# Turning the token rows of a sparse expert block: two TensorE transposes into one half of PSUM and two ScalarE copies, or four TensorE matmuls into both halves and one copy

## The chip, the cores and the metric

The kernel runs on one core of a Trainium2 chip. The metric is the time of one execution on the device in microseconds (us), as the median of several runs. The engines are named as in the profile: PE is TensorE's matmuls, PEld its weight loads, DVE is VectorE, ACT is ScalarE, POOL is GpSimd, SP is SyncE.

## What is computed

The model is a chain of eight stages on a tensor of 8 x 32 x 32 pixels with 64 channels: a spatial stage and then a mixture of experts, four times over. The change lies in the last two mixtures, `ffn2` and `ffn3`, which compute the same function with different weights. Each normalised token goes to the best two of eight experts; an expert is a gated network of width 682:

```python
    def _L2_ffn_ref(x, router_w, w1, w2, w3):
        N_EXPERTS = 8
        TOP_K = 2
        B, T, C = x.shape
        flat = x.reshape(-1, C)
        logits = flat @ router_w.T
        probs = jax.nn.softmax(logits, axis=-1)
        topk_probs, topk_idx = jax.lax.top_k(probs, TOP_K)
        topk_probs = topk_probs / (jnp.sum(topk_probs, axis=-1, keepdims=True) + 1e-09)
        onehot = jax.nn.one_hot(topk_idx, N_EXPERTS, dtype=flat.dtype)
        gates = jnp.einsum('nk,nke->ne', topk_probs, onehot)
        h1 = jnp.einsum('nc,ehc->neh', flat, w1)
        h3 = jnp.einsum('nc,ehc->neh', flat, w3)
        h = jax.nn.silu(h1) * h3
        y = jnp.einsum('neh,ech->nec', h, w2)
        out = jnp.einsum('ne,nec->nc', gates, y)
        return out.reshape(B, T, C)
...
    x = x + _L2_conv_ref(_ln_c(x), ...)
    t = _to_tokens(x)
    t = t + _L2_ffn_ref(_ln_t(t), L2_ffn_router_w, L2_ffn_w1, L2_ffn_w2, L2_ffn_w3)
    x = _from_tokens(t, x)
    x = x + _L3_conv_ref(_ln_c(x), ...)
    t = _to_tokens(x)
    t = t + _L3_ffn_ref(_ln_t(t), L3_ffn_router_w, L3_ffn_w1, L3_ffn_w2, L3_ffn_w3)
```

## The kernel before

Both stages are built by `sparse_stage`. Its first part normalises the tokens, chooses experts and scatters every token's row, with its gate, into regions of DRAM by expert. Its second part, the one that the change touches, works through `SLOT_BLOCKS` = 71 blocks of 256 rows, each block with one expert's weights; there are 142 blocks in the two stages. All operands are float32.

A block b is done in these steps, with the line numbers of the profile:

- `turn_x` (L1251): the 256 rows lie in `xin` as two tiles of 128 rows by 64 channels. Each tile is transposed on TensorE, with the identity as moving operand, into the PSUM tile `x_ps`, partitions 0 to 63. The rows are the stationary operand.
- `copy_x` (L1310 and L1311): ScalarE copies those 64 partitions twice into `turned` in SBUF, once to partitions 0 to 63 and once to 64 to 127. Both halves are needed because the two up-projections, w1 and w3, lie in the two halves of the partitions of `weights` and are multiplied by the two halves of TensorE's rows.
- `up(b, c)` for c = 0, 1, 2 (L1262): each call is four matmuls of 64 rows by 114 columns, with 256 moving columns: two chunks of hidden units, and for each w1 and w3.
- ScalarE takes Silu of the first product (L1320) and VectorE multiplies it by the second (L1350), which gives `hidden`.
- `downs(b)` (L1273): six matmuls of 114 rows by 64 columns, alternately into partitions 0 to 63 and 64 to 127 of `y_ps`. VectorE copies the sums to `y_half` (L1331).
- `fold(b)` (L1284): two matmuls of the full array that turn the result back and add the halves; VectorE multiplies by the gates (L1338), and GpSimd scatters the rows to DRAM (L1241).

The order on TensorE is written out by hand: for each b it is `up(b, 0)`, `up(b, 1)`, `turn_x(b + 1)`, `fold(b - 2)`, `up(b, 2)`, `downs(b - 1)`. On ScalarE the copy for block b + 1 stands between the Silu of c = 1 and that of c = 2. `up(b, 0)` waits for `x_copied`, `up(b, c)` for the `hidden` of two steps before, since there are two PSUM buffers.

In the trace an `up`, `downs` or `fold` matmul shows as two MATMUL records, each with its own weight load, and a transpose as one: L1251 has 284 records for 284 transposes, L1284 has 568 for 284 matmuls. "128*64" in a row is rows by columns of the array that are in use, "128x128" behind it the moving operand.

Of the kernel before, what the change touches and what calls it, by code (L numbers as in the profile page):

```python
# [15 lines left out]
P = 128  # L16
BATCH, SIDE, CH = 8, 32, 64
# [731 lines left out]
BLOCK = SUB * P  # L749
HELD = 26  # L750
# [56 lines left out]
def sparse_stage(nc, sem, k, name):  # L807
    dram = k.dram
    blocks_of_rows = k.slots.rearrange("(b p j) c -> b p j c", p=P, j=SUB)
    with ExitStack() as ctx:  # L810
# [18 lines left out]
        with ExitStack() as inner:  # L829
            def sbi(n, shape, dt=F32):  # L830
                return inner.enter_context(nc.sbuf_tensor(f"{name}_{n}", shape, dt))

            def psi(n, shape):
                return inner.enter_context(nc.psum_tensor(f"{name}_{n}", shape, F32))
# [14 lines left out]
            turned, kept, multiplied, placed, rows_set = (  # L849
                sem(f"{name}_{n}") for n in ("turned", "kept", "multiplied", "placed", "rows_set"))  # L850
# [304 lines left out]
        with ExitStack() as inner:  # L1155
# [3 lines left out]
            def psi(n):  # L1159
# [4 lines left out]
            x_ps, out_ps = psi("x_ps"), psi("out_ps")  # L1164
            y_ps = [psi(f"y_ps{i}") for i in (0, 1)]
            xin = sbi("xin", [P, HELD, SUB, ROW])
            turned = sbi("turned", [P, 2, BLOCK])
# [7 lines left out]
            x_turned, x_copied, up_done, silu_done, hidden_done = (  # L1175
                sem(f"{name}_{n}") for n in ("x_turned2", "x_copied", "up_done", "silu_done", "hidden_done"))
# [69 lines left out]
            @block.tensor  # L1246
            def _(pe):
                def turn_x(b):
                    pe.wait_ge(x_loaded[b % HELD], 16 * (b // HELD + 1))
                    for j in range(SUB):  # L1250
                        last = nc.tensor.transpose(x_ps[0:CH, j * P:(j + 1) * P], xin[:, b % HELD, j, 0:CH],  # L1251
                                                   k.ident[:, :])
                    last.then_inc(x_turned, 1)

                def up(b, c):
                    n = PAIRS_C * b + c
                    if n >= 2:
                        pe.wait_ge(hidden_done, n - 1)
                    for chunk in (2 * c, 2 * c + 1):
                        for w in (0, 1):  # L1260
                            rows_of = slice(w * CH, (w + 1) * CH)
                            last = nc.tensor.matmul(up_ps[w][n % 2][0:SIZE,  # L1262
                                                                    chunk % 2 * BLOCK:(chunk % 2 + 1) * BLOCK],
                                                    weights[rows_of, b % WEIGHTS, chunk * SIZE:(chunk + 1) * SIZE],
                                                    turned[rows_of, b % 2, :], start=True, stop=True)
                    last.then_inc(up_done, 1)

                def downs(b):
                    pe.wait_ge(hidden_done, PAIRS_C * (b + 1))
                    for c in range(CHUNKS):  # L1270
                        half = c % 2
                        col = UP_COLS + c * CH
                        last = nc.tensor.matmul(y_ps[b % 2][half * CH:(half + 1) * CH, 0:BLOCK],  # L1273
                                                weights[0:SIZE, b % WEIGHTS, col:col + CH],
                                                hidden[0:SIZE, b % 2, c // 2, c % 2 * BLOCK:(c % 2 + 1) * BLOCK],
                                                start=(c < 2), stop=(c >= CHUNKS - 2))
                    last.then_inc(down_done, 1)

                def fold(b):
                    pe.wait_ge(y_kept, b + 1)  # L1280
                    if b > 0:
                        pe.wait_ge(y_ready, b)
                    for j in range(SUB):
                        last = nc.tensor.matmul(out_ps[:, j * CH:(j + 1) * CH],  # L1284
                                                y_half[:, b % 2, j * P:(j + 1) * P], k.fold[:, :],
                                                start=True, stop=True)
                    last.then_inc(folded, 1)

                turn_x(0)
                for b in range(SLOT_BLOCKS):  # L1290
                    pe.wait_ge(x_copied, b + 1)
                    pe.wait_ge(w_loaded[b % WEIGHTS], 16 * (b // WEIGHTS + 1))
                    up(b, 0)
                    up(b, 1)
                    if b + 1 < SLOT_BLOCKS:
                        turn_x(b + 1)
                    if b >= 2:
                        fold(b - 2)
                    up(b, 2)
                    if b >= 1:  # L1300
                        downs(b - 1)
                downs(SLOT_BLOCKS - 1)
                fold(SLOT_BLOCKS - 2)
                fold(SLOT_BLOCKS - 1)

            @block.scalar
            def _(act):
                def copy_x(b):
                    act.wait_ge(x_turned, b + 1)
                    nc.scalar.copy(turned[0:CH, b % 2, :], x_ps[0:CH, 0:BLOCK])  # L1310
                    nc.scalar.copy(turned[CH:P, b % 2, :], x_ps[0:CH, 0:BLOCK]).then_inc(x_copied, 1)  # L1311

                copy_x(0)
                for b in range(SLOT_BLOCKS):
                    for c in range(PAIRS_C):
                        n = PAIRS_C * b + c
                        act.wait_ge(up_done, n + 1)
                        if n >= 2:
                            act.wait_ge(hidden_done, n - 1)
                        nc.scalar.activation(silu[0:SIZE, n % 2, :], up_ps[0][n % 2][0:SIZE, :],  # L1320
                                             ACT.Silu).then_inc(silu_done, 1)
                        if c == 1 and b + 1 < SLOT_BLOCKS:
                            copy_x(b + 1)
# [1939 lines left out]
```

## Time and profile before

| | |
|---|---|
| median of 3 runs | 2289.25 us (2287.74 to 2291.01) |
| time of the profiled execution | 2279.4 us |
| span of the profile | 2277.6 us |
| mean granted TensorE clock (1.0 is full speed) | 0.839 |
| PE busy | 1677.3 us (74%), 11157 records |
| PEld busy | 967.5 us (42%) |
| DVE busy | 1245.0 us (55%) |
| ACT busy | 965.8 us (42%) |
| L1262 PE, `up` | 445.8 us busy, 3408 records |
| L1273 PE, `downs` | 215.2 us busy, 1704 records |
| L1284 PE, `fold` | 79.7 us busy, 568 records |
| L1251 PE, `turn_x` | 58.6 us busy, 284 records |
| L1310 ACT, the first copy | 50.1 us busy, 142 |

The profile is of one execution, whose time is 2 us more than its span and 10 us less than the median. Busy shares are means over eight unlike stages; what the change is worth is read from the blocks, whose turns run from 1273.1 us, at the start of `ffn2`, to 2236.1 us, in `ffn3`, with the `sht` stage between. Ends of matmuls in the trace are modelled, so durations of neighbouring groups overlap; starts are the better measure.

### The profile page before, as it was taken

How to read it: one execution, taken by the hardware profiler on the slowest of the kernel's cores; microseconds unless marked ns; L12 is line 12 of the kernel's file. 1: busy time of each engine (PE TensorE's matmuls, PEld its weight loads, DVE VectorE, ACT ScalarE, POOL GpSimd, SP SyncE). 2: the span in 40 equal slices, each digit the busy share in tenths (PEclk: the TensorE clock that was granted, in tenths of full speed). 3: DMA queues.
4: the chain of work that ended last, by engine and by line, in shares of the span. 5: the costliest groups of instructions: out<-in, count | busy, mean ns of one | idle time of the engine just before them, and what ended most of it. 6: DMA issues, size and time to landing. Idle time of an engine off the chain costs nothing. (4 is left out here: it accounts for less than half of the span.)

```text
span 2277.6 us, 30440 instructions
## 1 busy us (share of the span) xinstructions
PE 1677.3 (74%) x11157; PEld 967.5 (42%) x11157; DVE 1245.0 (55%) x2416; ACT 965.8 (42%) x1715; POOL 590.1 (26%) x591
## 2 busy tenths in 40 slices
PE   2899996897999970312304599999845539999994
PEld 2433333345333340100103366666545426666663
DVE  6643335655633357578787555555462565555554
ACT  2565653333655543325123244444322424444441
POOL 0100000001000000000005577743452157776332
PEclk8899997996999975556555799999967759999997
DMA  1322210002222200000000354444268014544444
GB/s 41 76 68 65 65 56 20 0 0 50 76 65 65 65 23 0 0 0 0 0 4 27 117 147 147 149 138 134 92 152 167 7 57 149 147 146 143 133 133 151
DMA packets 117333, 175.30 MB, mean 77 GB/s; under 512 B 38106, under 2 KB 66522, under 8 KB 116674
## 3 DMA queue, kind: packets, MB, share of 16 engines
q1 hardware_dynamic: 99906, 155.38, 23.8%
q0 software_dynamic: 17280, 17.99, 2.4%
q8 instruction: 89, 1.46, 0.3%
q14 instruction: 58, 0.48, 0.1%
HBM read 148.60 MB, written 24.70 MB: 76 GB/s over the span
## 5 line engine op out<-in xcount | busy, mean ns | idle before, releaser
L1350 DVE TENSOR_TENSOR ffn_hidden<-ffn_silu,ffn_up_ps 114x512 f32<-114x512 f32 x426 | 293.0, 688 | 349.9 <-ACT ffn_silu L1320 349.0
L1262 PE MATMUL ffn_up_ps<-ffn_turned,ffn_weights 64*114 64x256 f32 x3408 | 445.8, 394 | 5.8 <-DMA ffn_weights<-in_ffn_weights 4.9
L1320 ACT ACTIVATE ffn_silu<-ffn_up_ps 114x512 f32<-114x512 f32 x426 | 254.4, 597 | 388.9 <-PE ffn_up_ps L1262 386.5
L826 POOL DMA_INDIRECT slots<-ffn_rows,ffn_slot x256 | 251.7, 983 | 557.4 <-DVE ffn_slot L944 386.4
L736 ACT ACTIVATE ffn_hidden<-ffn_up_ps,ffn_b 128x512 f32<-128x512 f32 x512 | 310.1, 689 | 198.0 <-PE ffn_up_ps L631 198.0
L1241 POOL DMA_INDIRECT results<-ffn_yout,ffn_xin x284 | 271.9, 957 | 246.0 <-DVE ffn_yout L1338 179.6
L1262 PEld LDWEIGHTS ffn_up_ps<-ffn_turned,ffn_weights 64*114 64x114 f32 x3408 | 288.1, 176 | 110.6 <-issue 59.6
L631 PE MATMUL ffn_up_ps<-ffn_T,ffn_up_w 64*128 64x512 f32 x1024 | 261.2, 623 | 3.1 <-ACT ffn_hidden L736 3.1
L652 PE MATMUL ffn_y_ps<-ffn_hidden,ffn_down 128*64 128x512 f32 x1024 | 247.9, 605 | 3.4 <-DVE ffn_y_total L526 3.4
L1273 PE MATMUL ffn_y_ps<-ffn_hidden,ffn_weights 114*64 114x256 f32 x1704 | 215.2, 388 | 0.0
L526 DVE SCALAR_TENSOR_TENSOR ffn_gated<-ffn_y_ps,ffn_b,ffn_gates 128x512 f32<-128x512 f32 x96 | 72.0, 751 | 204.7 <-PE ffn_y_ps L652 203.1
L631 PEld LDWEIGHTS ffn_up_ps<-ffn_T,ffn_up_w 64*128 64x128 f32 x1024 | 91.5, 188 | 168.5 <-ACT ffn_hidden L736 92.9
L1273 PEld LDWEIGHTS ffn_y_ps<-ffn_hidden,ffn_weights 114*64 114x64 f32 x1704 | 109.7, 136 | 89.9 <-DVE ffn_hidden L1350 48.2
L652 PEld LDWEIGHTS ffn_y_ps<-ffn_hidden,ffn_down 128*64 128x64 f32 x1024 | 62.3, 136 | 161.6 <-ACT ffn_hidden L736 85.3
L1251 PE MATMUL ffn_x_ps<-ident,ffn_xin 128*64 128x128 f32 x284 | 58.6, 289 | 48.0 <-DMA ffn_xin<-slots 48.0
L526 DVE SCALAR_TENSOR_TENSOR ffn_y_total<-ffn_y_ps,ffn_b,ffn_gates 128x512 f32<-128x512 f32 x32 | 23.7, 750 | 113.4 <-PE ffn_y_ps L652 92.0
L1057 PE MATMUL ffn_turn_ps<-ident,D 128*128 128x128 f32 x64 | 17.3, 431 | 89.8 <-DVE D L879 89.8
L1284 PE MATMUL ffn_out_ps<-fold,ffn_y_half 128*128 128x64 f32 x568 | 79.7, 263 | 1.4 <-DVE ffn_y_half L1331 1.4
L1284 PEld LDWEIGHTS ffn_out_ps<-fold,ffn_y_half 128*128 128x128 f32 x568 | 74.6, 191 | 3.2 <-DVE ffn_y_half L1331 1.7
L2724 POOL MEMSET hyp_ones<- 128x128 f32 x1 | 0.2, 204 | 288.7 <-POOLq L3096 288.7
L2138 PE MATMUL dc_conv_ps<-dc_fresh,dc_step_w 128*128 128x512 f32 x144 | 67.6, 617 | 8.8 <-DVE dc_fresh L2124 8.8
L1310 ACT COPY ffn_turned<-ffn_x_ps 64x256 f32<-64x256 f32 x142 | 50.1, 353 | 56.0 <-PE ffn_x_ps L1251 56.0
(412 smaller groups left out, 2067.1 us busy)
## 6 DMA issues: line engine op xcount, KB each, us to landing
ffn_weights<-in_ffn_weights SPq DMA_DIRECT2D x142, 534.0 KB
ffn_gates<-gate_rows SPq DMA_DIRECT2D x128, 256.0 KB
ffn_xin<-slots SPq DMA_DIRECT2D x142, 66.0 KB
sht_mix<-in_sht_weights SPq DMA_DIRECT2D x8, 1024.0 KB, 8.4
results<-ffn_yout,ffn_xin POOLq DMA_INDIRECT x284
slots<-ffn_rows,ffn_slot POOLq DMA_INDIRECT x256
D<-results SPq DMA_DIRECT2D x16, 256.0 KB, 5.4
ffn_second<-results SPq DMA_DIRECT2D x16, 256.0 KB, 5.9
```

What stands on the lines that cost most here:

```text
L526: nc.vector.scalar_tensor_tensor(target, y_ps[th][:, :], b2[:, p:p + 1], gates[:, n % GATES, th, :], ALU.add, ALU.mult).then_inc(y_gated, 1)
L631: nc.tensor.matmul(up_ps[j][:, :], up_w[rows, 2 * p + half, c * P:(c + 1) * P], T[rows, g * NTOK:(g + 1) * NTOK], start=True, stop=True).t ...
L652: last = nc.tensor.matmul(y_ps[th][rows, :], down[:, 2 * p + half, c, :], hidden[:, n % 2 * UNITS + 2 * half + th, :], start=(c == 0), sto ...
L736: nc.scalar.activation(hidden[:, n % 2 * UNITS + j, :], up_ps[j][:, :], ACT.Gelu, bias=b1[:, bias_at:bias_at + 1], scale=1.0).then_inc(hid ...
L826: nc.gpsimd.indirect_dma_start(k.slots, bass.IndirectOffsetOnAxis(slot[c][:, t:t + 1], 0), rows[c][:, t, :], None).then_inc(row_stored[h], 16)
L1241: nc.gpsimd.indirect_dma_start(k.results, bass.IndirectOffsetOnAxis(xin[:, b % HELD, j, CH + 1:CH + 2].bitcast(I32), 0), yout[:, b % HELD, ...
L1262: last = nc.tensor.matmul(up_ps[w][n % 2][0:SIZE, chunk % 2 * BLOCK:(chunk % 2 + 1) * BLOCK], weights[rows_of, b % WEIGHTS, chunk * SIZE:( ...
L1273: last = nc.tensor.matmul(y_ps[b % 2][half * CH:(half + 1) * CH, 0:BLOCK], weights[0:SIZE, b % WEIGHTS, col:col + CH], hidden[0:SIZE, b % ...
L1284: last = nc.tensor.matmul(out_ps[:, j * CH:(j + 1) * CH], y_half[:, b % 2, j * P:(j + 1) * P], k.fold[:, :], start=True, stop=True)
L1320: nc.scalar.activation(silu[0:SIZE, n % 2, :], up_ps[0][n % 2][0:SIZE, :], ACT.Silu).then_inc(silu_done, 1)
L1350: nc.vector.tensor_tensor(hidden[0:SIZE, b % 2, c, :], silu[0:SIZE, n % 2, :], up_ps[1][n % 2][0:SIZE, :], ALU.mult).then_inc(hidden_done, 1)
L2138: last = nc.tensor.matmul(bank[:, :], step_w[:, g, dx, :], fresh[slot][:, :, dx:dx + SIDE], start=False, stop=(dx == 2), skip_group_check= ...
```

## The change

`turn_x` issues an ordinary matmul with the identity in place of each transpose, and issues it twice, with the output in partitions 0 to 63 and in 64 to 127 of `x_ps`. `copy_x` then copies all 128 partitions in one instruction.

```diff
                 def turn_x(b):
                     pe.wait_ge(x_loaded[b % HELD], 16 * (b // HELD + 1))
                     for j in range(SUB):
-                        last = nc.tensor.transpose(x_ps[0:CH, j * P:(j + 1) * P], xin[:, b % HELD, j, 0:CH],
-                                                   k.ident[:, :])
+                        for half in (0, 1):
+                            last = nc.tensor.matmul(x_ps[half * CH:(half + 1) * CH, j * P:(j + 1) * P],
+                                                    xin[:, b % HELD, j, 0:CH], k.ident[:, :], start=True, stop=True)
                     last.then_inc(x_turned, 1)
...
                 def copy_x(b):
                     act.wait_ge(x_turned, b + 1)
-                    nc.scalar.copy(turned[0:CH, b % 2, :], x_ps[0:CH, 0:BLOCK])
-                    nc.scalar.copy(turned[CH:P, b % 2, :], x_ps[0:CH, 0:BLOCK]).then_inc(x_copied, 1)
+                    nc.scalar.copy(turned[:, b % 2, :], x_ps[:, 0:BLOCK]).then_inc(x_copied, 1)
```

On TensorE's queue a block now reads like this, from the turn for block 12 in `ffn2` to the last `up` of block 11; names in brackets are the semaphores that a row waits for, and "64x128" is the output's shape:

```order
L1251 MATMUL ffn_x_ps<-ident,ffn_xin 64x128 [waits ffn2_x_loaded12]
L1251 MATMUL ffn_x_ps<-ident,ffn_xin 64x128
L1284 MATMUL ffn_out_ps<-fold,ffn_y_half 128x64 [waits ffn2_y_ready,ffn2_y_kept]
L1284 MATMUL ffn_out_ps<-fold,ffn_y_half 128x64
L1262 MATMUL ffn_up_ps<-ffn_turned,ffn_weights 114x256 [waits ffn2_hidden_done]
L1262 MATMUL ffn_up_ps<-ffn_turned,ffn_weights 114x256 x3
```

The same place in the changed kernel, whose lines are numbered one higher:

```order
L1252 MATMUL ffn_x_ps<-ident,ffn_xin 64x128 [waits ffn2_x_loaded12]
L1252 MATMUL ffn_x_ps<-ident,ffn_xin 64x128 x3
L1285 MATMUL ffn_out_ps<-fold,ffn_y_half 128x64 [waits ffn2_y_ready,ffn2_y_kept]
L1285 MATMUL ffn_out_ps<-fold,ffn_y_half 128x64
L1263 MATMUL ffn_up_ps<-ffn_turned,ffn_weights 114x256 [waits ffn2_hidden_done]
L1263 MATMUL ffn_up_ps<-ffn_turned,ffn_weights 114x256 x3
```

Two instructions have become four ahead of the fold; the order around them, and what each row waits for, is the same.

## Rows read from the trace of the kernel before

**Rows 1.** The page: PE's busy tenths in 40 slices, and the last chain by engine.

```profile
PE   2899996897999970312304599999845539999994
...
PE 16%; DMA 1%; DVE 0%; SPq 0%; issue 0%; POOL 0%; POOLq 0%; ACT 0%
```

**Rows 2.** Busy time by engine in ten blocks of `ffn3`, with the clock.

```profile
core 0: us, PE busy (x) PEld busy (x) DVE busy (x) ACT busy (x) POOL busy (x), PEclk, DMA share, GB/s
1889.34:1940.81 51.47, 51.47 (x422) 34.48 (x422) 26.89 (x50) 24.06 (x50) 38.97 (x42) 1.00 0.51 147
```

**Rows 3.** Timeline of PE, one block: start, duration to the modelled end, what.

```profile
1930.44 1.99 PE L1262 MATMUL ffn_up_ps<-ffn_turned,ffn_weights 64*114 64x256 f32 x16
1932.36 0.41 PE L1251 MATMUL ffn_x_ps<-ident,ffn_xin 128*64 128x128 f32 x2
1932.61 0.56 PE L1284 MATMUL ffn_out_ps<-fold,ffn_y_half 128*128 128x64 f32 x4
1933.09 1.12 PE L1262 MATMUL ffn_up_ps<-ffn_turned,ffn_weights 64*114 64x256 f32 x8
1934.14 1.52 PE L1273 MATMUL ffn_y_ps<-ffn_hidden,ffn_weights 114*64 114x256 f32 x12
1935.59 1.99 PE L1262 MATMUL ffn_up_ps<-ffn_turned,ffn_weights 64*114 64x256 f32 x16
```

**Rows 4.** Timeline of ACT in the same block; idle time before a row in brackets.

```profile
1932.97 0.35 ACT L1310 COPY ffn_turned<-ffn_x_ps 64x256 f32<-64x256 f32 x1
1933.34 0.36 ACT L1311 COPY ffn_turned<-ffn_x_ps 64x256 f32<-64x256 f32 x1
1934.26 0.60 ACT L1320 ACTIVATE ffn_silu<-ffn_up_ps 114x512 f32<-114x512 f32 x1 [0.56 <-PE ffn_up_ps L1262]
```

**Rows 5.** Timeline of DVE in the same block: `hidden` of c = 0.

```profile
1932.24 0.69 DVE L1350 TENSOR_TENSOR ffn_hidden<-ffn_silu,ffn_up_ps 114x512 f32<-114x512 f32 x1 [1.26 <-ACT ffn_silu L1320]
```

**Rows 6.** Timeline of PE, `ffn2`'s last block, which has no turn.

```profile
1639.35 0.66 PE L1284 MATMUL ffn_out_ps<-fold,ffn_y_half 128*128 128x64 f32 x4
1639.97 1.12 PE L1262 MATMUL ffn_up_ps<-ffn_turned,ffn_weights 64*114 64x256 f32 x8
1641.02 3.00 PE L1273 MATMUL ffn_y_ps<-ffn_hidden,ffn_weights 114*64 114x256 f32 x24
1643.96 0.66 PE L1284 MATMUL ffn_out_ps<-fold,ffn_y_half 128*128 128x64 f32 x4
```

**Rows 7.** Timeline of PE in `ffn0`: full-array matmuls, then column halves.

```profile
126.39 2.00 PE L664 MATMUL ffn_out_ps<-fold,ffn_y_total 128*128 128x64 f32 x16
128.32 1.08 PE L652 MATMUL ffn_y_ps<-ffn_hidden,ffn_down 128*64 128x512 f32 x4
```

**Rows 8.** Timeline of PE in the `sht` stage: transposes (L1861) and matmuls (L1871).

```profile
1779.47 0.60 PE L1861 MATMUL sht_modes_ps<-ident,sht_lat 128*128 128x128 f32 x4
1779.90 1.06 PE L1871 MATMUL sht_out_ps<-sht_inverse,sht_modes 128*128 128x128 f32 x8
1780.80 0.60 PE L1861 MATMUL sht_modes_ps<-ident,sht_lat 128*128 128x128 f32 x4
```

**Rows 9.** Four lines on PE: duration of one record, ns, min/median/max.

```profile
L1251 PE MATMUL ffn_x_ps<-ident,ffn_xin x284: 272/297/423, 1273.1 to 2236.1; 128*64 128x128 f32 x142
...
L1273 PE MATMUL ffn_y_ps<-ffn_hidden,ffn_weights x1704: 379/379/431, 1286.0 to 2245.5; 114*64 114x256 f32 x190
...
L1801 PE MATMUL sht_spec_ps<-sht_forward_leg,sht_fourier x256: 270/273/445, 1697.4 to 1744.7; 128*32 128x128 f32 x128
...
L652 PE MATMUL ffn_y_ps<-ffn_hidden,ffn_down x1024: 592/592/886, 88.5 to 816.0; 128*64 128x512 f32 x171
```

**Rows 10.** Timeline of PE at the start of `ffn2`.

```profile
1276.19 3.76 PE L1262 MATMUL ffn_up_ps<-ffn_turned,ffn_weights 64*114 64x256 f32 x16 [2.48 <-DMA ffn_weights<-in_ffn_weights]
...
1284.63 0.41 PE L1251 MATMUL ffn_x_ps<-ident,ffn_xin 128*64 128x128 f32 x2
1284.97 1.12 PE L1262 MATMUL ffn_up_ps<-ffn_turned,ffn_weights 64*114 64x256 f32 x8
```

## The prediction

> **What bounds the kernel now.** I read the page first: PE shows nine tenths or more through both stretches of blocks, and the last chain is 16% PE against 1% for anything else [rows 1]. A busy PE can still hide waiting, so I went to the windows: in ten blocks of `ffn3` PE is busy for all 51.47 us at full clock (1.00, the 2.4 GHz level), DVE and ACT for about half of it [rows 2]. So a block takes 5.15 us, as the starts of two neighbouring blocks say too, 1930.44 and 1935.59 [rows 3]. Both other engines wait for PE: ACT stood idle for 0.56 us until the Silu of c = 2 had its product [rows 4], and DVE for 1.26 us behind ACT [rows 5]. What counts is therefore the time that TensorE's queue takes, piece by piece, and the timeline of PE gives it by starts: `up` 1.92, turn 0.25 (1932.36 to 1932.61), fold 0.48 (to 1933.09), `up` 1.05, `downs` 1.45 [rows 3].
>
> **What the rows say about the array.** Three things are needed to price the new turn.
>
> First, a slot. Sixteen `up` records take 1.99 us and eight take 1.12 [rows 3], so eight take 0.87. Alone on the full array, matmul records of 128 columns follow each other every 0.11 us (eight from 1779.90 to 1780.80) and transposes every 0.108 (four from 1779.47 to 1779.90) [rows 8]. Records of 256 columns should need 0.217 each, 1.74 for eight; they need half, because w1 and w3 sit in different row halves and run side by side. So a slot of 256 columns is 0.217 us and one of 128 is 0.109.
>
> Second, whether column halves overlap too, which the new turn needs. `ffn0` has the same pattern: four records of 512 columns, one matmul to each column half, take 1.08 us [rows 7]. A record lasts 0.592 [rows 9] and its slot is 4 x 0.109 = 0.436; one after another the last would end at 3 x 0.436 + 0.592 = 1.90, in two slots at 0.436 + 0.592 = 1.03. It is two slots, plus 0.05 for a first weight load that nothing hides. `downs` agrees: five slots of 0.217 and a last record of 0.379 [rows 9] make 1.46, measured 1.52 [rows 3], so 0.06 for that load.
>
> Third, the change of shape. Where row halves, column halves and the full array follow each other, the next group starts 0.06 to 0.08 us before the modelled end of the last record: `up` to turn (1930.44 + 1.99 against 1932.36), fold to `up`, `downs` to `up` [rows 3], full array to column halves (126.39 + 2.00 against 128.32) [rows 7], column halves to fold (1641.02 + 3.00 against 1643.96) [rows 6]. I call this a drain and use 0.07. Today the turn passes to the fold without one: the fold starts 0.16 before the turn's modelled end and takes 0.56 in all [rows 3], and so do transposes and full-array matmuls in `sht` (1779.47 + 0.60 against 1779.90) [rows 8]. After a drain a fold takes 0.66 [rows 6], because its first weight load is no longer covered.
>
> **The change part by part.** Removed on PE: two transposes, one record each. Added: four matmuls of two records, so eight records of 128 columns, four in each column half, in four slots. From the turn's start: 0.06 for the first load, three slots of 0.109, then the last record. Its length is that of a 128-column record in column tiles, 0.27 (the median of L1801; the shortest of L1251 is the same) [rows 9]. That is 0.66 to its modelled end; less 0.07, the fold starts 0.59 after the turn, where it starts 0.25 after it now. The drain ahead of the turn is there already and stays. The fold comes after a drain now: 0.66 less 0.07, so the next `up` starts 0.59 after it, where it is 0.48 now. Turn and fold together: 0.59 + 0.59 = 1.18, now 0.73, so **0.45 us more per block**.
>
> Each stage has 70 turns in its loop, and 68 of them stand before a fold: 136 x 0.45 = 61.2 us. The first two turns in each loop have no fold behind them. At the warm one `up` starts 0.34 after the turn [rows 10], and it would be 0.59 then; four times 0.25 is 1 us, somewhat more where the clock is still low. The turn ahead of each loop costs nothing: `up` waits 2.48 us for its weights there [rows 10], and the added matmuls, about half a microsecond at the low clock, fit in.
>
> Removed on ACT: one copy of 0.36 us in each block [rows 4], 51 us in all. I put this at nothing. The second copy ends at 1933.70 [rows 4] and the `up` that needs it starts at 1935.59 [rows 3], 1.89 later; ACT is idle for half of a block and its next Silu waits for PE in any case. The copy of 128 partitions is not in the trace; between nothing and twice the present 0.36 it ends long before that `up`. Behind it on ACT stands the Silu of c = 2, which will be 0.45 later with PE. The other waits get slacker: `up(b, 2)` needs the `hidden` that ends at 1932.93 [rows 5] and starts at 1933.09 [rows 3], so PE is the later already, and nothing is added for DVE, GpSimd or the DMAs.
>
> Sum: 61.2 + 1 = 62 us. The profiled execution took 2279.4, so it would take 2341.6. The median is 10 us above that execution, and I add the same 62 to it: **2351 us**, 2.7% slower. A change under 0.2%, some 5 us, could not be told from none.
>
> **A rule weighed against the rows.** An ordinary matmul streams two records where a transpose streams one, at equal 0.11 per 128 columns [rows 8]: twice the time. The Trainium skill, page "TensorE: Matmul & The Clock Gate", section "Terms", says that transpose mode is four times faster for FP32. By that the four matmuls would need eight slots even with both halves side by side, and the total would be that of the second rival; the rows bear out twice, so the sum stays.
>
> **The rivals.**
> - No drain behind the turn, as with the transposes today. Then the fold starts after 0.06 + 4 x 0.109 = 0.50 and takes 0.48: 0.25 more per block, 35 us, 2324 us. Against it: column halves to fold does drain [rows 6]. A matmul with the identity that is run as a transpose all the same, one record per half, comes to nearly the same: 0.06 + 0.109 + 0.27 - 0.07 + 0.59 = 0.96, 0.23 more, 2321 us. Nothing in the rows speaks for it.
> - The halves do not overlap, as each matmul to half 64 to 127 stands behind one that reads the same rows as weights. Eight slots in place of four add 4 x 0.109 = 0.44: 0.89 per block, 122 us, 2411 us. Against it: the same alternation in `ffn0` and in `downs` [rows 3, 7].
> - Not slower: the x copies set the start of the next block. Then the turn's end, 0.34 later, is paid back by one copy of 0.36: 0.02 less per block, 2286 us, no change that can be told. It decides only where the second copy ends later than `downs`, so it would have to be 1.9 us later than it is [rows 3, 4].
>
> **How the numbers follow.** The forecast gets 0.80; slot, load and drain are each known to about 0.01 us, so with some play for the first blocks and for the step from the profiled execution to a median it reaches from 2342 to 2362. The cheaper turn gets 0.08, the dearer one 0.09 (0.02 of it for the rule of four), the copies 0.03. The range 2330 to 2370 takes the whole of the first and room for a drain or a load of half or twice the size, and leaves the three others out, 0.20 together. Slower: 0.80 + 0.08 + 0.09 = 0.97; same 0.02 and faster 0.01 share the last.
>
> **What would show it.** In the profile after: 1136 records on the turn's line in place of 284, about 0.27 us each; a block of 5.60 us on PE's timeline; the fold 0.59 after the turn, starting about 0.07 before its modelled end, and 0.66 long; clock 1.00 in the blocks; one copy of 128x256 per block, ACT's busy time some 50 us less, and its idle time before the Silu of c = 2 about 0.7 longer. A fold that starts before the last turn record is 0.2 old would show the first rival, starts of the two halves 0.11 apart and never together the second. What would make the forecast wrong: PE idle inside a block today that the modelled ends hide, or a shape of matmul that drains between its own halves.

## The result and the profile after

The changed kernel takes 2349.66 us, the median of four runs (2348.55 to 2352.92), against 2289.25 before: a ratio of 1.027, with a 95% interval of 1.0256 to 1.0285. The forecast was 2351 us, slower. Ratios and their intervals, here and below, are estimates from all the runs and not quotients of two medians, from which they differ a little. A fourth run of the kernel before took 7328.6 us, far from all others, and is not in its median.

The page of the changed kernel: busy time by engine, PE's tenths in 40 slices, the last chain by engine, and the lines of the turn, the fold and the copy (busy time, mean ns of one, idle time before).

```profile
PE 1747.8 (74%) x12009; PEld 1014.2 (43%) x12009; DVE 1244.5 (53%) x2416; ACT 928.5 (39%) x1573; POOL 589.6 (25%) x591
...
PE   2899996888999941211223999999665539999994
...
PE 17%; DMA 1%; DVE 0%; SPq 0%; issue 0%; POOL 0%; POOLq 0%; ACT 0%
...
L1252 PE MATMUL ffn_x_ps<-ident,ffn_xin 128*64 128x128 f32 x1136 | 94.8, 288 | 48.1 <-DMA ffn_xin<-slots 48.1
...
L1285 PE MATMUL ffn_out_ps<-fold,ffn_y_half 128*128 128x64 f32 x568 | 93.5, 287 | 1.4 <-DVE ffn_y_half L1331 1.4
...
L1311 ACT COPY ffn_turned<-ffn_x_ps 128x256 f32<-128x256 f32 x142 | 52.8, 372 | 57.5 <-PE ffn_x_ps L1252 57.5
```

PE is as full as before, 74% of a longer span, and still holds the chain [rows 1]. The turn's line has 1136 records where 284 stood, and the fold's line, which was not edited, went from 79.7 to 93.5 us. To put the place of the loss beyond doubt, here are the two stretches of blocks, each from its first turn into its last fold, in windows with the busy time of the engines, the clock and the DMA share. First the changed kernel:

```profile
core 0: us, PE busy (x) PEld busy (x) DVE busy (x) ACT busy (x) POOL busy (x), PEclk, DMA share, GB/s
...
1281.92:1685.40 403.48, 399.83 (x3408) 265.67 (x3408) 190.64 (x354) 154.18 (x285) 221.75 (x233) 0.99 0.41 128
1918.30:2321.30 403.00, 399.13 (x3408) 265.29 (x3408) 190.66 (x354) 154.18 (x285) 221.67 (x232) 0.99 0.42 128
```

And the same two stretches of the kernel before:

```profile
1273.07:1645.70 372.63, 368.87 (x2981) 246.20 (x2982) 190.77 (x354) 172.28 (x356) 221.85 (x233) 0.99 0.45 139
1875.75:2247.50 371.75, 368.30 (x2981) 245.78 (x2982) 190.75 (x354) 172.21 (x356) 221.66 (x232) 0.99 0.45 139
```

The stretches grew by 30.85 and 31.25 us, 62.1 together, at the same mean granted clock of 0.99. PE's busy time in them grew by 30.96 and 30.83, so nothing of this is a new wait. ACT has 18 us less to do in each, and the time does not show it.

The timeline of PE in the changed kernel, at the start of `ffn2`, to be laid beside [rows 10], and in one block, beside [rows 3]:

```profile
1285.42 3.76 PE L1263 MATMUL ffn_up_ps<-ffn_turned,ffn_weights 64*114 64x256 f32 x16 [2.38 <-DMA ffn_weights<-in_ffn_weights]
...
1293.87 0.66 PE L1252 MATMUL ffn_x_ps<-ident,ffn_xin 128*64 128x128 f32 x8
1294.45 1.12 PE L1263 MATMUL ffn_up_ps<-ffn_turned,ffn_weights 64*114 64x256 f32 x8
...
1938.46 1.99 PE L1263 MATMUL ffn_up_ps<-ffn_turned,ffn_weights 64*114 64x256 f32 x16
1940.37 0.66 PE L1252 MATMUL ffn_x_ps<-ident,ffn_xin 128*64 128x128 f32 x8
1940.96 0.66 PE L1285 MATMUL ffn_out_ps<-fold,ffn_y_half 128*128 128x64 f32 x4
1941.55 1.12 PE L1263 MATMUL ffn_up_ps<-ffn_turned,ffn_weights 64*114 64x256 f32 x8
1942.60 1.52 PE L1274 MATMUL ffn_y_ps<-ffn_hidden,ffn_weights 114*64 114x256 f32 x12
1944.05 1.99 PE L1263 MATMUL ffn_up_ps<-ffn_turned,ffn_weights 64*114 64x256 f32 x16
```

In the block, by starts: `up` 1.91, turn 0.59 (was 0.25), fold 0.59 (was 0.48), `up` 1.05, `downs` 1.45. A block takes 5.59 us where it took 5.15. The turn ends 0.07 after the fold's start, and the fold takes 0.66 in all, as after column halves in [rows 6]. At the start, `up` follows the warm turn after 0.58 (was 0.34), and the wait for weights still covers the turn ahead of the loop, 2.38 us where it was 2.48.

The timeline of ACT in that block, to be laid beside [rows 4]:

```profile
1940.49 0.60 ACT L1320 ACTIVATE ffn_silu<-ffn_up_ps 114x512 f32<-114x512 f32 x1 [0.27 <-PE ffn_up_ps L1263]
1941.08 0.37 ACT L1311 COPY ffn_turned<-ffn_x_ps 128x256 f32<-128x256 f32 x1
1942.72 0.60 ACT L1320 ACTIVATE ffn_silu<-ffn_up_ps 114x512 f32<-114x512 f32 x1 [1.27 <-PE ffn_up_ps L1263]
```

One copy of 128 partitions takes 0.37, hardly longer than one of 64 did (0.35 and 0.36). The time that it saves went straight into the wait for the next product, together with PE's delay: 1.27 us where 0.56 stood.

### The profile page after: what moved, and what is told of

It reads as the page before. It is cut to its first block and busy times, and to the rows that moved or that the text cites. A ratio compares the mean times of both kernels' runs of the same rounds, so it can differ in the third digit from the quotient of the medians.

```text
span 2351.0 us, 32002 instructions
## 1 busy us (share of the span) xinstructions
PE 1747.8 (74%) x12009; PEld 1014.2 (43%) x12009; DVE 1244.5 (53%) x2416; ACT 928.5 (39%) x1573; POOL 589.6 (25%) x591
## 5 line engine op out<-in xcount | busy, mean ns | idle before, releaser
L652 PE MATMUL ffn_y_ps<-ffn_hidden,ffn_down 128*64 128x512 f32 x1024 | 247.8, 605 | 3.5 <-DVE ffn_y_total L526 3.5
L652 PEld LDWEIGHTS ffn_y_ps<-ffn_hidden,ffn_down 128*64 128x64 f32 x1024 | 62.4, 136 | 161.5 <-ACT ffn_hidden L736 85.4
L1252 PE MATMUL ffn_x_ps<-ident,ffn_xin 128*64 128x128 f32 x1136 | 94.8, 288 | 48.1 <-DMA ffn_xin<-slots 48.1
L1252 PEld LDWEIGHTS ffn_x_ps<-ident,ffn_xin 128*64 128x64 f32 x1136 | 60.0, 137 | 98.9 <-DMA ffn_xin<-slots 50.4
L1285 PE MATMUL ffn_out_ps<-fold,ffn_y_half 128*128 128x64 f32 x568 | 93.5, 287 | 1.4 <-DVE ffn_y_half L1331 1.4
L1311 ACT COPY ffn_turned<-ffn_x_ps 128x256 f32<-128x256 f32 x142 | 52.8, 372 | 57.5 <-PE ffn_x_ps L1252 57.5
```

The costliest lines, as they stand in the source:

```text
L652: last = nc.tensor.matmul(y_ps[th][rows, :], down[:, 2 * p + half, c, :], hidden[:, n % 2 * UNITS + 2 * half + th, :], start=(c == 0), sto ...
L1252: last = nc.tensor.matmul(x_ps[half * CH:(half + 1) * CH, j * P:(j + 1) * P], xin[:, b % HELD, j, 0:CH], k.ident[:, :], start=True, stop=True)
L1285: last = nc.tensor.matmul(out_ps[:, j * CH:(j + 1) * CH], y_half[:, b % 2, j * P:(j + 1) * P], k.fold[:, :], start=True, stop=True)
```

## The experiments

The theory: PE alone sets the time of a block. A slot is the time from the start of one record to that of the next on the same part of the array. Half of the loss is slots (four of 128 columns where two were), the other half the change of shape between the turn and the fold, with the uncovered weight loads on both sides of it; the second half of the partitions and the copies weigh nothing. The rivals of the prediction split the same sum in other ways: halves one behind the other, a turn without a drain, copies that matter.

**The copy alone.** The transposes stay, and one copy takes all 128 partitions. The upper half of `x_ps` is filled only once, with block 0's rows, and holds them for all later blocks; so the time is that of the copy edit, but the w3 products are those of block 0's rows. The diff is against the kernel before.

```diff
...
                     for j in range(SUB):
+                        if b == 0:
+                            nc.tensor.matmul(x_ps[CH:P, j * P:(j + 1) * P], xin[:, b % HELD, j, 0:CH],
+                                             k.ident[:, :], start=True, stop=True)
                         last = nc.tensor.transpose(x_ps[0:CH, j * P:(j + 1) * P], xin[:, b % HELD, j, 0:CH],
...
                     act.wait_ge(x_turned, b + 1)
-                    nc.scalar.copy(turned[0:CH, b % 2, :], x_ps[0:CH, 0:BLOCK])
-                    nc.scalar.copy(turned[CH:P, b % 2, :], x_ps[0:CH, 0:BLOCK]).then_inc(x_copied, 1)
+                    nc.scalar.copy(turned[:, b % 2, :], x_ps[:, 0:BLOCK]).then_inc(x_copied, 1)
```

> ScalarE's part of the change alone: the two transposes stay, one copy of 128 partitions replaces the two copies. It leaves out that the second half of the copied rows is that of their block: it holds block 0's rows throughout, so the products with w3 are wrong. My theory: the copies end 1.89 us before the matmul that needs them, so a block stays at 5.15 us and the time at 2290 us, within 3 us. The rival, that the copies set the start of the next block: 0.36 us less in each of 142 blocks, 51 us, 2239 us.

Measured: 2289.01 us (ten runs, 2280.08 to 2290.81) against 2288.11 before, ratio 1.0003 (0.9986 to 1.0019). Its timeline of ACT, one copy and the Silu behind it:

```profile
1942.92 0.37 ACT L1313 COPY ffn_turned<-ffn_x_ps 128x256 f32<-128x256 f32 x1
1944.21 0.60 ACT L1322 ACTIVATE ffn_silu<-ffn_up_ps 114x512 f32<-114x512 f32 x1 [0.92 <-PE ffn_up_ps L1265]
```

The copy that fell away, 0.36 us, came back as wait: the Silu waits 0.92 us for PE where it waited 0.56 [rows 4]. So the ScalarE half of the change, done without the other, is worth nothing that can be measured: the rival of copies that matter, 2239 us, is out.

**The matmuls alone.** The four matmuls of the changed kernel, with the two copies of the kernel before. The diff is against the changed kernel, here and in the next three.

```diff
-                    nc.scalar.copy(turned[:, b % 2, :], x_ps[:, 0:BLOCK]).then_inc(x_copied, 1)
+                    nc.scalar.copy(turned[0:CH, b % 2, :], x_ps[0:CH, 0:BLOCK])
+                    nc.scalar.copy(turned[CH:P, b % 2, :], x_ps[0:CH, 0:BLOCK]).then_inc(x_copied, 1)
```

> TensorE's part of the change alone: four matmuls into both halves, but the two copies of before, both from the lower half, so that the upper half of the PSUM tile is written for nothing. My theory: the time of the changed kernel, 2350 us within 3, with a block of 5.59 us, since the saved copy pays nothing there either. The rival, that the saved copy pays for part of the matmuls: up to 51 us more than the changed kernel, 2400 us.

Measured: 2349.59 us (2346.88 to 2351.29), ratio 1.0262 (1.0243 to 1.0281). That is the changed kernel's time, and PE's timeline is the changed kernel's too (turn to fold 0.59, fold to `up` 0.59, a block 5.59). The whole loss is TensorE's.

**Two matmuls, to one half.** The matmuls to the upper half are left out, and the two copies are back.

```diff
-                        for half in (0, 1):
-                            last = nc.tensor.matmul(x_ps[half * CH:(half + 1) * CH, j * P:(j + 1) * P],
-                                                    xin[:, b % HELD, j, 0:CH], k.ident[:, :], start=True, stop=True)
+                        last = nc.tensor.matmul(x_ps[0:CH, j * P:(j + 1) * P], xin[:, b % HELD, j, 0:CH],
+                                                k.ident[:, :], start=True, stop=True)
...
-                    nc.scalar.copy(turned[:, b % 2, :], x_ps[:, 0:BLOCK]).then_inc(x_copied, 1)
+                    nc.scalar.copy(turned[0:CH, b % 2, :], x_ps[0:CH, 0:BLOCK])
+                    nc.scalar.copy(turned[CH:P, b % 2, :], x_ps[0:CH, 0:BLOCK]).then_inc(x_copied, 1)
```

> Only the transposes replaced: two ordinary matmuls into the lower half in place of two transposes, and the two copies of before. My theory: the four records in one column half need the same four slots as four records in each of two, and the drain ahead of the fold is there too, so it is as slow as the changed kernel, 2350 us, with a turn of 0.59 us and a fold of 0.66. The rival, that the second half costs slots of its own: about half of the added time, 2320 us.

Measured: 2346.65 us (2340.11 to 2351.27), ratio 1.025 (1.0221 to 1.0278), an interval that overlaps the changed kernel's. Its timeline of PE:

```profile
1940.65 0.65 PE L1251 MATMUL ffn_x_ps<-ident,ffn_xin 128*64 128x128 f32 x4
1941.23 0.66 PE L1284 MATMUL ffn_out_ps<-fold,ffn_y_half 128*128 128x64 f32 x4
1941.82 1.12 PE L1262 MATMUL ffn_up_ps<-ffn_turned,ffn_weights 64*114 64x256 f32 x8
```

Four records take 0.65 us where eight take 0.66. The second half is free within 0.01 us, and the prediction's second rival (halves one behind the other) is out. It also says where the loss begins: with the step from a transpose to a matmul, even with as many instructions as before and in the same half.

**Slots without the change of shape.** Each transpose is issued twice into the same place, with the two copies. That makes four records of 128 columns per block, as many slots as the changed kernel's eight records in two halves take.

```diff
-                        for half in (0, 1):
-                            last = nc.tensor.matmul(x_ps[half * CH:(half + 1) * CH, j * P:(j + 1) * P],
-                                                    xin[:, b % HELD, j, 0:CH], k.ident[:, :], start=True, stop=True)
+                        for again in (0, 1):
+                            last = nc.tensor.transpose(x_ps[0:CH, j * P:(j + 1) * P], xin[:, b % HELD, j, 0:CH],
+                                                       k.ident[:, :])
...
-                    nc.scalar.copy(turned[:, b % 2, :], x_ps[:, 0:BLOCK]).then_inc(x_copied, 1)
+                    nc.scalar.copy(turned[0:CH, b % 2, :], x_ps[0:CH, 0:BLOCK])
+                    nc.scalar.copy(turned[CH:P, b % 2, :], x_ps[0:CH, 0:BLOCK]).then_inc(x_copied, 1)
```

> Slots without the drain: each transpose of the kernel before is issued twice, to the same place, so four records of 128 columns in four slots, in the shape that passes to the fold without a drain. My theory: 2 more slots of 0.109 us per block and nothing else, 0.22 in 140 turns, 31 us, 2320 us, with the fold still 0.48 ahead of the next up. The rival, that all of the change's cost is slots and a drain is free: 0.45 per block, 2350 us.

Measured: 2321.51 us (2319.19 to 2323.96), ratio 1.0141 (1.0121 to 1.0162). Its timeline of PE:

```profile
1941.32 0.63 PE L1252 MATMUL ffn_x_ps<-ident,ffn_xin 128*64 128x128 f32 x4
1941.78 0.56 PE L1285 MATMUL ffn_out_ps<-fold,ffn_y_half 128*128 128x64 f32 x4
1942.27 1.12 PE L1263 MATMUL ffn_up_ps<-ffn_turned,ffn_weights 64*114 64x256 f32 x8
...
1946.69 0.63 PE L1252 MATMUL ffn_x_ps<-ident,ffn_xin 128*64 128x128 f32 x4
```

The turn is about as long as in the changed kernel (0.63 against 0.66), but the fold starts 0.46 after it and not 0.59, and needs 0.49 and not 0.59: it starts 0.17 before the modelled end of the turn, and its first load lies under the turn (the weight load starts at 1941.68, 0.10 ahead of the fold's first record; in the changed kernel it starts with the fold, at 1940.96). A block takes 5.37. So of the 0.44 us that a block lost, 0.22 are two more slots and 0.22 the change of shape with its loads. In the total: 33 us of slots (2321.51 less 2288.11), 28 of the rest (2349.59 with the matmuls alone, less 2321.51).

**The matmuls where the shape does not change.** The changed kernel's turn is put behind `downs`, which also writes to column halves, two blocks ahead; the copy moves with it, and on SP's queue the rows are loaded ahead of the weights.

```diff
...
-                        load_weights(experts[b - first], b)
                         if b > 0:
                             load_x(places[b - first], b)
+                        load_weights(experts[b - first], b)
...
                 turn_x(0)
+                pe.wait_ge(x_copied, 1)
+                turn_x(1)
                 for b in range(SLOT_BLOCKS):
...
                     up(b, 1)
-                    if b + 1 < SLOT_BLOCKS:
-                        turn_x(b + 1)
                     if b >= 2:
...
                         downs(b - 1)
+                    if b + 2 < SLOT_BLOCKS:
+                        pe.wait_ge(x_copied, b + 2)
+                        turn_x(b + 2)
...
```

> The drain of the change undone by place: the four matmuls of the changed kernel stand right behind the down-projections, which use the same column halves, and turn two blocks ahead; the fold stands alone between the ups. (Rows are loaded ahead of the weights of the same block, so that they are there.) My theory: no drain between downs and turn, whose first weight load is covered, so the turn costs its four slots, 0.44 us; the fold keeps its drains, and the up behind it waits 0.03 for the product of c = 0, as in the block without a turn today. A block of 1.92 + 0.62 + 1.05 + 1.45 + 0.44 = 5.48 us, 0.33 over the kernel before, 46 us, 2335 us. The rival, that place does not matter and only the added records cost: a block of 5.59 us, 2350 us.

Measured: 2332.85 us (2330.28 to 2335.64) against 2286.92 before, ratio 1.0213 (1.0183 to 1.0242). Its timeline of PE:

```profile
1945.09 1.99 PE L1263 MATMUL ffn_up_ps<-ffn_turned,ffn_weights 64*114 64x256 f32 x16
1947.01 0.66 PE L1285 MATMUL ffn_out_ps<-fold,ffn_y_half 128*128 128x64 f32 x4
1947.64 1.12 PE L1263 MATMUL ffn_up_ps<-ffn_turned,ffn_weights 64*114 64x256 f32 x8
1948.69 1.52 PE L1274 MATMUL ffn_y_ps<-ffn_hidden,ffn_weights 114*64 114x256 f32 x12
1950.03 0.61 PE L1252 MATMUL ffn_x_ps<-ident,ffn_xin 128*64 128x128 f32 x8
1950.57 1.99 PE L1263 MATMUL ffn_up_ps<-ffn_turned,ffn_weights 64*114 64x256 f32 x16
```

The turn starts 1.34 after `downs`, where `up` started 1.45 after it, and takes 0.61 where it took 0.66, with its first load covered. A block takes 5.48 us (1945.09 to 1950.57), 0.11 less than in the changed kernel, and the kernel loses 46 us and not 60. The same instructions, one change of shape fewer. Behind `downs` the turn starts 0.18 before the modelled end of the last record, so an ordinary matmul does not drain where the shape stays. The price of a change is not one number, though: this block has as many slots and as many changes as the one with doubled transposes and takes 0.11 more (5.48 against 5.37), mostly because the fold, now behind an `up`, takes 0.63 by starts and not 0.49.

**The kernel before with fewer changes of shape.** If a change costs 0.12 us or so, the kernel before pays for four in each block. Here its transposes and copies stay, and blocks go in pairs, so that `downs` stands between two `up` and the turns and folds of two blocks stand together: six changes in two blocks where eight were. `x_ps` and `out_ps` hold two blocks, `turned` three, and the rows are loaded ahead of the weights. ScalarE's and VectorE's orders, not shown, follow. The diff is against the kernel before.

```diff
...
+                for b in range(1, SLOT_BLOCKS, 2):
+                    start(b)
                     up(b, 0)
                     up(b, 1)
-                    if b + 1 < SLOT_BLOCKS:
-                        turn_x(b + 1)
-                    if b >= 2:
-                        fold(b - 2)
+                    downs(b - 1)
                     up(b, 2)
-                    if b >= 1:
-                        downs(b - 1)
+                    start(b + 1)
+                    up(b + 1, 0)
+                    if b + 2 < SLOT_BLOCKS:
+                        turn_x(b + 2)
+                        turn_x(b + 3)
+                    if b >= 2:
+                        fold(b - 2, b - 2)
+                    fold(b - 1, b - 2)
+                    up(b + 1, 1)
+                    up(b + 1, 2)
+                    downs(b)
...
```

> The lesson turned round, from the kernel before with its transposes and two copies: fewer changes of shape. Blocks go in pairs: up(b,0) up(b,1), downs(b-1), up(b,2) up(b+1,0), both turns and both folds of a pair together, up(b+1,1) up(b+1,2), downs(b); so six changes of shape in two blocks where there are eight. My theory, from starts in the trace: a pair takes 3 x 1.92 for the ups, 2 x 1.45 for the downs, and 0.47 + 0.93 for four transposes and eight fold records, 10.06 us where two blocks take 10.29; 35 pairs in each stage save 16 us, 2273 us. The rival, that a drain costs nothing and records alone count: the same 2289 us. A third: the rows or products of a pair come too late and the ups wait, which would show as idle PE, and slower than before.

Measured: 2278.93 us (twelve runs, 2269.76 to 2286.55) against 2286.92 before (seventeen runs), ratio 0.997 (0.9954 to 0.9987). It is faster than the kernel before, but by 8 us only, where its forecast had 16. Its timeline of PE: a turn in `ffn2` for which the rows came late, with the `up` behind it; a pair as most are in `ffn3`; and one there in which the rows came late.

```profile
1410.13 0.41 PE L1251 MATMUL ffn_x_ps<-ident,ffn_xin 128*64 128x128 f32 x2 [2.39 <-DMA ffn_xin<-slots]
...
1411.31 1.99 PE L1262 MATMUL ffn_up_ps<-ffn_turned,ffn_weights 64*114 64x256 f32 x16
...
1942.18 0.62 PE L1251 MATMUL ffn_x_ps<-ident,ffn_xin 128*64 128x128 f32 x4
1942.65 1.00 PE L1284 MATMUL ffn_out_ps<-fold,ffn_y_half 128*128 128x64 f32 x8
1943.58 1.99 PE L1262 MATMUL ffn_up_ps<-ffn_turned,ffn_weights 64*114 64x256 f32 x16
1945.50 1.52 PE L1273 MATMUL ffn_y_ps<-ffn_hidden,ffn_weights 114*64 114x256 f32 x12
1946.94 1.99 PE L1262 MATMUL ffn_up_ps<-ffn_turned,ffn_weights 64*114 64x256 f32 x16
1948.86 1.52 PE L1273 MATMUL ffn_y_ps<-ffn_hidden,ffn_weights 114*64 114x256 f32 x12
1950.31 1.99 PE L1262 MATMUL ffn_up_ps<-ffn_turned,ffn_weights 64*114 64x256 f32 x16
1952.22 0.63 PE L1251 MATMUL ffn_x_ps<-ident,ffn_xin 128*64 128x128 f32 x4
...
2006.04 0.41 PE L1251 MATMUL ffn_x_ps<-ident,ffn_xin 128*64 128x128 f32 x2 [2.78 <-DMA ffn_xin<-slots]
2006.29 1.20 PE L1284 MATMUL ffn_out_ps<-fold,ffn_y_half 128*128 128x64 f32 x8
2007.42 3.42 PE L1262 MATMUL ffn_up_ps<-ffn_turned,ffn_weights 64*114 64x256 f32 x16
```

A pair takes 10.04 us (1942.18 to 1952.22) where two blocks took 10.29: 0.25 less for two changes fewer, so 0.12 each, near the 0.11 that the run before saved by one, and about half of the 0.22 that the change between turn and fold costs. Over 70 pairs that would be 17 us. Part of it is lost where the second turn of a pair has to wait for its rows: 2.39 us once in `ffn2`, 2.78 once in `ffn3`. Both times the rows are those of block 26, by the order of the loads, and a pair turns that block one block earlier than before. The chain that led to the second wait shows why they were late:

```profile
1995.01 2.41 DMA slots<-ffn_rows,ffn_slot
...
1998.46 2.70 SPq L1192
...
2001.18 2.77 SPq L1192
...
2004.13 1.86 DMA ffn_xin<-slots
```

SP's queue waited for the last scatter into `slots` before it loaded the rows of block 25; then it read its tables of places and experts for the next 13 blocks (L1192, 2.70 and 2.77 us), and only then asked for block 26, whose rows took 1.86 us to land. The second wait costs more than itself, as the windows around it show, the first of them in the wait:

```profile
2004.00:2006.00 2.00, 0.00 (x0) 0.00 (x0) 0.29 (x1) 0.00 (x0) 1.70 (x2) 1.00 0.44 120
2007.42:2010.70 3.28, 3.28 (x17) 2.35 (x16) 1.04 (x3) 1.16 (x3) 2.45 (x3) 0.55 0.15 50
2012.00:2014.00 2.00, 2.00 (x20) 1.37 (x16) 0.63 (x2) 0.60 (x1) 1.39 (x3) 1.00 0.37 110
```

Behind it the mean granted clock is 0.55, almost all of it at the 1.2 GHz level, and the same 16 records take 3.42 us in place of 1.99; then it is 1.00 again. Behind the wait of 2.39 in `ffn2` it is not so: there the 16 records take 1.99. From the first turn to the start of the last fold the two stages take 366.1 and 367.2 us, against 372.3 and 371.4 before: 10.3 of the 17 us. The two waits, that slow group and two shorter waits for rows (0.39 and 0.26) are 7.2 us, which covers what is missing. A version that keeps the pairs and has these rows loaded earlier was not tried, nor was the new order on SP's queue alone.

## Why the prediction was right

**PE sets the time.** It does: the stretches of blocks grew by as much as PE's busy time in them, and one copy in place of two, taken alone, changed nothing.

**The slot and the column halves.** The turn was to start its fold after 0.59 us and did. Two halves to a slot, read from `ffn0` [rows 7], is shown by the run with two matmuls, where half the records took the same time.

**The drain.** This was the disputed step: today the turn passes to the fold without one, and the same row shape, 128*64, stands before both. The forecast said that the turn as a matmul in a column half would drain like `downs` before a fold [rows 6]. The doubled transposes show it: with as many slots, 0.22 us per block hang on which instruction stands ahead of the fold. That it is the shape and not the matmul as such is shown by the turn behind `downs`, which starts 0.18 before the modelled end, and by [rows 8], where full-array matmuls pass to transposes 0.16 before theirs. The forecast's two prices came out as well: 0.34 us more at the turn and 0.11 at the fold.

The Trainium skill, page "TensorEngine Tiling (Array Packing)", section "Key Properties", says that changing the tiling mode drains the engine. The trace agrees: a step between row halves, column halves and the full array costs 0.11 to 0.22 us here, drain and uncovered weight load together. The Trainium skill, page "TensorEngine Tiling (Array Packing)", section "Restrictions", says that column tiling rules out the FP32 transpose mode. The trace is consistent with it: the transposes, though of 64 columns, pass to the full-array fold without a drain.

**The matmul at twice a transpose, not four times.** Two matmuls (0.65 us) take what four transposes take (0.63). The prediction weighed a rule against this: the Trainium skill, page "TensorE: Matmul & The Clock Gate", section "Terms", says that transpose mode is four times faster for FP32. The trace differs: it is twice here, and the measurement decides.

**The copies at nothing.** Right in the time. The forecast of ACT's busy time, some 50 us less, was too large: it fell by 37. The step that failed is that the two old copies counted in full. Here is the line of ACT's timeline of the kernel before that stands ahead of [rows 4]:

```profile
1932.48 0.60 ACT L1320 ACTIVATE ffn_silu<-ffn_up_ps 114x512 f32<-114x512 f32 x1 [0.27 <-PE ffn_up_ps L1262]
```

The Silu ends at 1933.08 and the first old copy started at 1932.97, so 0.11 us of it lay under the Silu; the new copy, whose turn ends later, starts as the Silu ends. Its 0.37 replaces 0.62 that counted: 0.25 in each of 142 blocks, 36 us. That the copies are worth nothing did not rest on it.

**The sum.** 62 us forecast, 62.1 measured in the blocks; a block grew by 0.44 and not 0.45, within what two decimals of a start allow. Between the two profiled executions the difference is 73.4 us (spans of 2277.6 and 2351.0), and the other 11 are outside the blocks, in stages that the change doesn't touch: the first turn starts at 1281.92 and not at 1273.07, and the stretch between `ffn2` and `ffn3` is 232.9 and not 230.05. In the six other kernels the first turn starts at 1281.2 to 1284.2 too, or at 1277.2 in the one with the turn behind `downs`, so it is the profiled execution of before that was short there. The traces say where: in the window from 70 to 90 us, in `ffn0`, its mean granted clock was 0.92, and in the changed kernel's 0.50 (0.50 to 0.59 in the six others); `ffn0`'s first down-projection (L652) starts at 88.50 and at 96.68, 8.2 us apart. Up to there the two kernels issue the same work, and why the clock rose earlier in one execution stays open. Adding the loss to the median, and not to that execution's own 2279.4, brought the forecast within 1.4 us; 2341.6 would have been 8 too low. The prediction gave no reason for the gap of 10 us, so that step was an assumption that held.

## What to carry to other kernels

Before a copy is saved on one engine at the price of instructions on another, see in the timeline which of the two the next block waits for: here 37 us less work on ScalarE only made its waits longer, and 62 us more on TensorE went into the time one for one. On TensorE, count the changes between row halves, column halves and the full array as instructions of their own (0.11 to 0.22 us each here, so by estimate half a microsecond for the four in a 5.15 us block), and let steps of one shape stand together. When such a regrouping makes a transfer due earlier, see what stands ahead of it in its queue: of the two waits that came of it here, the one of 2.78 us was followed by 16 records at the low clock, and the one of 2.39 was not.

## What was not expected of the hardware

A second matmul into the other column half, forecast to be free, costs next to nothing indeed: 0.66 us for eight records, 0.65 for four. A copy of 128 partitions takes hardly longer than one of 64 (0.372 and 0.353 to 0.364 us for 256 columns). In the paired kernel the clock stood at 1.00 through the last 2 us of TensorE's idle time, and was at 0.55 only in the work behind it.
